# P.V issued for two chunks at a time, four column sums on TensorE, maxima split by reductions alone

## The chip, the cores and the metric

The kernel runs on one core of one Trainium2 chip. The core's engines work side by side and meet only at semaphores: TensorE (PE in the profile, its weight loads PEld), VectorE (DVE), ScalarE (ACT), GpSimd (POOL) and SyncE (SP), which issues the DMAs here. The metric is the time of one execution in device microseconds. Before the change the median of three runs is 5370.73 us (5370.23 to 5371.38).

## The reference

A post-norm transformer layer on x of 4 x 2048 x 512 in fp32, with 16 heads of 32:

```
q, k, v = x @ Wq.T + bq, x @ Wk.T + bk, x @ Wv.T + bv       # 16 heads of 32
scores  = q k^T / sqrt(32) + bias                           # bias: -inf in 3 columns of 2048
attn    = softmax(scores);  ctx = attn @ v
y  = layernorm(x + ctx @ Wo.T + bo) * gamma + beta
x1 = layernorm(x + y)
xq = quantize_4bit(x1 @ Hadamard);  wq = ternary(weight)
out = layernorm(x1 + xq @ wq.T)
```

The part that the change touches is the attention: softmax over 2048 keys for each of 2048 queries, 16 heads and 4 batches.

## The kernel before

Four batches run one after the other. A batch has 4 head groups of 4 heads, and a head group has 4 query blocks of 512 queries, so there are 16 blocks in a batch and 64 in all. After the 16 blocks of a batch comes a phase over its tokens (output projection, norms, quantised layer), which the change does not touch.

One block n works on 16 chunks of 128 keys. For a chunk c and each of the 4 heads, TensorE multiplies keys by queries (`score`, line 491, tile ps_s with NSB = 3 PSUM banks), ScalarE takes the exponential (line 679) into one of NPB = 6 buffers of `prob`, and TensorE adds the product with the values to ps_o (line 518, P.V). The four heads of P.V stand side by side on four strips of 32 columns of the array; scores use its whole width. The scores run one chunk ahead: while chunk c is in hand, the scores of c + 1 are issued, and in chunk 15 those of chunk 0 of the next block.

The sum of the exponentials over all keys is split. For the chunks of `PE_SUMS` TensorE multiplies them by ones (`column_sums`, line 496, ps_z, again on four strips). For the other chunks GpSimd adds the 128 x 2048 exponentials to `acc` (line 994), and at the end of the block TensorE sums `acc` too (the total), which waits for GpSimd's last addition. VectorE then takes the reciprocal (line 816) and GpSimd normalises (lines 978, 981) before it begins the next block's additions. A buffer of `prob` may be written again once its P.V (`pv`) and, for GpSimd's chunks, its addition (`padd`) are done (lines 676, 678).

The exponential needs the maximum of each query's scores before the block begins. So block n also computes the maxima for block n + 1: 64 units (`unit`, line 476), each a product of queries and 512 keys into one of NMB = 3 PSUM banks, of which VectorE takes the maximum (line 803). Unit u waits for the reduction of unit u - 3 (line 473). `unit_places` puts about five units into each of the chunks 1 to 13, one behind each score and two behind the last. Unit 0 waits for the stacked queries of block n + 1 (`q_stk`, line 468). When all 64 are reduced, VectorE combines them to 16 values per query row, negates them and splits them into a rounded high part and a rest (lines 805 to 810, `msplit`); TensorE transposes the two parts (line 483), ScalarE copies them (line 669), and two DMAs put them as rows into the stacked queries (line 321, `q_cur`). They take part in the score product, which so comes out with the maximum subtracted.

In chunk 14 TensorE also projects the queries of block n + 2 (`queries`, line 462, eight matmul records); ScalarE makes the high part (line 665), VectorE the low part (line 783), and SP issues three DMAs that stack them (line 285) and loads for the next projection. In front of the blocks 4, 8 and 12 of a batch (not 12 of the last batch) the keys and values of a head group are projected (lines 430, 436), about 30 us of TensorE. The last block of all has no units, since no block follows.

Every engine has its own program, written by hand in the order in which it runs; the order on TensorE within a block is that of `attend`.

Of the kernel before, what the change touches and what calls it, by code (L numbers as in the profile page):

```python
# [7 lines left out]
ALU = mybir.AluOpType  # L8
ACT = mybir.ActivationFunctionType
AX = mybir.AxisListType  # L10
F32 = mybir.dt.float32
F32R = mybir.dt.float32r
BF16 = mybir.dt.bfloat16

P = 128
NB, L, D = 4, 2048, 512
NH, HD = 16, 32
LBAND = 1024
TOPK = 3
HG = 4  # L20
# [4 lines left out]
NQB = L // QB  # L25
NKC = L // P
# [7 lines left out]
NPB = 6  # L34
# [1 line left out]
NBLK = NG * NQB  # L36
NSB, NMB = 3, 3

PE_SUMS = [2, 5, 8, 11, 14, 15]
POOL_SUMS = [c for c in range(NKC) if c not in PE_SUMS]  # L40
NADD = len(POOL_SUMS) - 1
ADD_OF = {c: max(i - 1, 0) for i, c in enumerate(POOL_SUMS)}
# [62 lines left out]
def build(nc, x, xT, wT, bqkv, woT, w_ffn, band, gamma, beta, bo, had, out):  # L105
# [3 lines left out]
    with ExitStack() as ctx:  # L109
        def sb(name, shape, dt=F32):  # L110
            return ctx.enter_context(nc.sbuf_tensor(name, shape, dt))

        def sem(name):
            return ctx.enter_context(nc.semaphore(name))
# [5 lines left out]
        vst = sb("vst", [P, 2, NKC, P])  # L120
        prob = sb("prob", [P, NPB, HG, QB])
# [8 lines left out]
        hi = sb("hi", [P, 2, QB], F32R)  # L130
        lo = sb("lo", [P, 2, QB], F32R)
        umax = sb("umax", [P, UNITS // NQB, NQB])
        negm = sb("negm", [P, HG * NQB])
        msplit = sb("msplit", [P, 2 * HG * NQB])
        mhi = sb("mhi", [P, HG * NQB], F32R)
        mrow = sb("mrow", [2 * HG * NQB, P], F32R)
        ident = sb("ident", [P, P])
        identb = sb("identb", [P, P], BF16)
# [31 lines left out]
        ps_o = ctx.enter_context(nc.psum_tensor("ps_o", [P, QB], F32))  # L170
# [50 lines left out]
        mstep = sem("mstep")  # L221
        mneg = sem("mneg")
# [3 lines left out]
        ex = sem("ex")  # L226
        pv = sem("pv")
        padd = sem("padd")
        zdone = sem("zdone")
        zrec = sem("zrec")  # L230
        oz_cp = sem("oz_cp")
# [194 lines left out]
        def _(pe):  # L426
# [30 lines left out]
            def queries(f):  # L457

                pe.wait_ge(wq_ld, (f + 1) * 16)
                pe.wait_ge(xq_ld, (f + 1) * 16)  # L460
                for c in range(IC):
                    mm = nc.tensor.matmul(ps_m[:, 0, :], wq[:, c], xq[:, c], start=c == 0, stop=c == IC - 1)  # L462
                mm.then_inc(qproj, 1)

            def unit(u, f, k, stage=None):

                if u == 0:
                    pe.wait_ge(q_stk, (f + 1) * NSTK)
                    if stage is not None:
                        for t in range(2):  # L470
                            pe.wait_ge(k_stk[t], (stage + 1) * (2 * NSTK))
                elif u >= NMB:
                    pe.wait_ge(mred, f * UNITS + u - NMB + 1)
                m, kb = divmod(u, NQB)
                h, qt = divmod(m, QB // P)
                nc.tensor.matmul(ps_m[:, u % NMB, :], qst[k % 2][0:RSTACK, h, qt * P:(qt + 1) * P],  # L476
                                 kst[k // NQB % 2][0:RSTACK, h, kb * QB:(kb + 1) * QB], start=True, stop=True).then_inc(msc, 1)

            def maxima_to_rows(f, first=False):
                if not first:  # L480
                    pe.wait_ge(q_cur, f * 32)
                pe.wait_ge(mneg, f + 1)
                nc.tensor.transpose(ps_m[0:2 * HG * NQB, 1, 0:P], msplit[:], ident[:]).then_inc(mtr, 1)

            def score(n, i, c, h, head=False):

                if c == 0 and h == 0:
                    pe.wait_ge(q_cur, (n + 1) * 32)
                if not head or h >= NSB:
                    pe.wait_ge(ex, n * (HG * NKC) + (HG * c + h - NSB + 1))  # L490
                nc.tensor.matmul(ps_s[:, (i * HG * NKC + HG * c + h) % NSB, :], kst[i // NQB % 2][0:RALL, h, c * P:(c + 1) * P],  # L491
                                 qst[i % 2][0:RALL, h, :], start=True, stop=True).then_inc(sc, 1)

            def column_sums(src, first, last):
                for h in range(HG):
                    mm = nc.tensor.matmul(ps_z[HD * h:HD * h + HD, :], ones[:, 0:HD], src[:, h, :], start=first, stop=last)  # L496
                return mm

            def attend(n, i, last):

                for c in range(NKC):
                    for h in range(HG):
                        if c < NKC - 1:
                            score(n, i, c + 1, h)
                        elif i < NBLK - 1:
                            score(n + 1, i + 1, 0, h)
                        for u in () if last and i == NBLK - 1 else units_at[c][h]:
                            unit(u, n + 1, i + 1, (n >> 2) + 1 if i % NQB == NQB - 1 else None)
                    if c == NKC - 2:
                        if not (last and i == NBLK - 1):  # L510
                            maxima_to_rows(n + 1)
                        if not (last and i >= NBLK - 2):
                            queries(n + 2)
                    if c == 0:
                        pe.wait_ge(oz_cp, n + 1)
                    pe.wait_ge(ex, n * (HG * NKC) + HG * c + HG)
                    for h in range(HG):
                        mm = nc.tensor.matmul(ps_o[HD * h:HD * h + HD, :], vst[:, i // NQB % 2, c, HD * h:HD * h + HD],  # L518
                                              prob[:, c % NPB, h, :], start=c == 0, stop=c == NKC - 1)
                    if c in PE_SUMS:  # L520
                        if c == PE_SUMS[0]:
                            pe.wait_ge(zrec, n + 1)
                        mm = column_sums(prob[:, c % NPB], c == PE_SUMS[0], False)
                    mm.then_inc(pv, 1)
                pe.wait_ge(padd, n * NADD + 2 * NADD)
                column_sums(acc, False, True).then_inc(zdone, 1)

# [79 lines left out]
            for oc in range(IC):  # L607
                mm = nc.tensor.matmul(ps_o[:, oc * P:(oc + 1) * P], ones[:], diag[:, oc * P:(oc + 1) * P], start=True, stop=True)
# [168 lines left out]
        def _(dve):  # L777
# [21 lines left out]
            def maxima(f):  # L799
                for u in range(UNITS):  # L800
                    dve.wait_ge(msc, f * UNITS + u + 1)
                    m, kb = divmod(u, NQB)
                    nc.vector.tensor_reduce(umax[:, m, kb:kb + 1], ps_m[:, u % NMB, :], AX.X, ALU.max).then_inc(mred, 1)  # L803
                dve.wait_ge(mred, (f + 1) * UNITS)
                nc.vector.tensor_reduce(negm[:], umax[:], AX.X, ALU.max, negate=True).then_inc(mstep, 1)
                dve.wait_ge(mstep, f * 2 + 1)
                nc.vector.tensor_copy(mhi[:], negm[:]).then_inc(mstep, 1)
                dve.wait_ge(mstep, f * 2 + 2)
                nc.vector.tensor_copy(msplit[:, 0:HG * NQB], mhi[:].bitcast(F32))
                nc.vector.tensor_tensor(msplit[:, HG * NQB:], negm[:], mhi[:].bitcast(F32), ALU.subtract).then_inc(mneg, 1)  # L810

            def inverse_sums(n):

# [290 lines left out]
```

## Time and profile before

| | |
|---|---|
| median of three runs | 5370.73 us (5370.23 to 5371.38) |
| the profiled execution | 5359.28 us, its span 5357.0 us |
| TensorE | 4980.8 us busy (93%), 25010 matmul records |
| VectorE | 3376.8 us (63%) |
| GpSimd | 3129.3 us (58%), 1103 instructions |
| ScalarE | 2590.8 us (48%) |
| granted TensorE clock | 0.976 of full speed on average; 1.00 in the blocks read below |
| a block without key projection | about 64.1 us from reciprocal to reciprocal |
| a block with it | about 94 to 97 us |
| the last block | 50.0 us |

A row of the timeline gives start and length in us, then engine, line, operation, output and input, the number of instructions merged in the row, and in brackets how long the engine was idle before it and what ended that. A busy TensorE need not be a fast one: where it alternates between kinds of matmul, or waits for a semaphore for a few tenths of a microsecond, the row of busy shares hides it. What a block costs has to be read from the distance between starts. Some matmul records of P.V and the sums count each matmul twice, as two passes.

### The profile page before, as it was taken

The numbers are of one execution on the slowest core, as the hardware profiler recorded it, in microseconds if no ns is written. First come the engines' busy times: TensorE is split into PE (matmuls) and PEld (weight loads), VectorE is DVE, ScalarE is ACT, GpSimd is POOL, SyncE is SP. The second block draws the span as 40 slices with busy tenths as digits, with TensorE's granted clock in tenths as the row PEclk, the third lists the DMA queues.
The fourth block names the chain that finished last, engine by engine and source line by source line (L and its number), as shares of the span: only waits on it lengthen the run. The fifth ranks groups of instructions, "written<-read, shape, count | busy, mean of one in ns | idle before, by whom it ended". The sixth has DMA issues, their size and how long they took to land.

```text
span 5357.0 us, 85355 instructions
## 1 busy us (share of the span) xinstructions
PE 4980.8 (93%) x25010; PEld 2442.2 (46%) x25048; DVE 3376.8 (63%) x5886; ACT 2590.8 (48%) x4891; POOL 3129.3 (58%) x1103
## 2 busy tenths in 40 slices
PE   6999999998889999999879999999988999999987
PEld 3444444443544444454344444444434444444434
DVE  5575756565766575756667666575766757567637
ACT  0454545453555454545345455454534545455545
POOL 1464656565566564656646566564664656566665
PEclk7999999999999999999989999999999999999988
DMA  4414131412411414131341221414133141321112
GB/s 113 93 37 95 37 78 37 95 36 76 112 36 37 95 37 95 37 78 39 89 113 37 51 63 39 93 37 95 37 90 96 36 95 36 72 54 42 36 40 73
DMA packets 247645, 346.36 MB, mean 65 GB/s; under 512 B 16529, under 2 KB 102289, under 8 KB 247186
## 3 DMA queue, kind: packets, MB, share of 16 engines
q1 hardware_dynamic: 247186, 340.73, 27.6%
q8 instruction: 228, 3.74, 0.3%
q14 instruction: 231, 1.89, 0.1%
HBM read 205.33 MB, written 33.55 MB: 45 GB/s over the span
## 4 chain that ended last, share of the span: by engine, by line
PE 74%; DMA 10%; POOL 5%; issue 4%; DVE 3%; ACT 2%; SPq 2%; POOLq 0%; ACTq 0%; DVEq 0%
PE ps_m L476 21%; PE ps_s L491 19%; PE ps_o L518 16%; DMA qst<-lo 7%; PE ps_z L496 5%; PE ps_m L462 4%; PE ps_m L430 3%; PE ps_m L436 2%; DMA xk<-in_xT_dram 2%; SPq L285 1%; ACT prob L679 1%; POOL prob L1020 1%; POOL prob L1024 1%; PE ps_s L436 1%; PE ps_s L430 1%
## 5 line engine op out<-in xcount | busy, mean ns | idle before, releaser
L803 DVE TENSOR_REDUCE umax<-ps_m 128x1 f32<-128x512 f32 x4096 | 2524.9, 683 | 753.3 <-PE ps_m L476 753.3
L679 ACT ACTIVATE prob<-ps_s 128x512 f32<-128x512 f32 x4096 | 2124.6, 601 | 1635.5 <-PE ps_s L491 1470.9
L994 POOL TENSOR_TENSOR acc<-acc,prob 128x2048 f32<-128x2048 f32 x512 | 2344.8, 4580 | 450.9 <-ACT prob L679 421.2
L491 PE MATMUL ps_s<-qst,kst 99*128 99x512 f32 x4096 | 1693.0, 430 | 126.1 <-ACT prob L679 69.4
L476 PE MATMUL ps_m<-kst,qst 97*128 97x512 f32 x4096 | 1699.7, 423 | 35.9 <-DMA qst<-lo 35.9
L491 PEld LDWEIGHTS ps_s<-qst,kst 99*128 99x128 f32 x4096 | 760.7, 190 | 1203.4 <-ACT prob L679 570.1
L518 PE MATMUL ps_o<-prob,vst 128*32 128x512 f32 x8192 | 1094.3, 606 | 0.0
L476 PEld LDWEIGHTS ps_m<-kst,qst 97*128 97x128 f32 x4096 | 780.7, 191 | 475.1 <-DVE umax L803 326.6
L994 POOL TENSOR_TENSOR acc<-prob 128x2048 f32<-128x2048 f32 x64 | 293.0, 4579 | 596.3 <-ACT prob L679 596.3
L978 POOL TENSOR_TENSOR obuf<-obuf,zinv 128x512 f32<-128x512 f32 x64 | 82.1, 1282 | 898.1 <-DVE zinv L816 898.1
L783 DVE SCALAR_TENSOR_TENSOR lo<-ps_m,bias,hi 128x512 fp32r<-128x512 f32 x116 | 87.1, 751 | 616.0 <-ACT hi L665 310.5
L816 DVE RECIPROCAL zinv<-ps_z 128x512 f32<-128x512 f32 x64 | 214.9, 3358 | 354.4 <-PE ps_z L496 354.4
L496 PE MATMUL ps_z<-prob,ones 128*32 128x512 f32 x3072 | 399.9, 592 | 0.0
L542 PE MATMUL ps_s<-vst,hi 128*128 128x512 f32 x512 | 238.5, 610 | 79.8 <-DMA hi<-ctxT_dram 79.8
L518 PEld LDWEIGHTS ps_o<-prob,vst 128*32 128x32 f32 x8192 | 161.9, 108 | 290.8 <-issue 177.0
L462 PE MATMUL ps_m<-xq,wq 128*128 128x512 f32 x512 | 235.7, 603 | 0.7 <-issue 0.7
L430 PE MATMUL ps_m<-xk,wkv 128*128 128x512 f32 x416 | 196.9, 618 | 31.4 <-DMA xk<-in_xT_dram 24.8
L436 PEld LDWEIGHTS ps_m<-wkv,xk 128*128 128x128 f32 x1664 | 194.0, 192 | 25.1 <-issue 25.1
L496 PEld LDWEIGHTS ps_z<-prob,ones 128*32 128x32 f32 x3072 | 99.9, 110 | 229.8 <-issue 229.8
L436 PE MATMUL ps_m<-wkv,xk 128*128 128x128 f32 x1664 | 194.2, 275 | 0.0
L542 PEld LDWEIGHTS ps_s<-vst,hi 128*128 128x128 f32 x512 | 96.4, 197 | 186.4 <-issue 102.1
L647 ACT ACTIVATE hi<-ps_m,bias 128x512 fp32r<-128x512 f32 x52 | 35.7, 687 | 243.0 <-PE ps_m L430 159.1
(105 smaller groups left out, 2341.9 us busy)
## 6 DMA issues: line engine op xcount, KB each, us to landing
xk<-in_xT_dram SPq DMA_DIRECT2D x66, 1024.0 KB, 7.7
xq<-in_xT_dram SPq DMA_DIRECT2D x65, 1024.0 KB, 8.9
kst<-hi SPq DMA_DIRECT2D x128, 256.0 KB, 9.2
qst<-hi SPq DMA_DIRECT2D x128, 256.0 KB, 5.6
wq<-in_wT_dram SPq DMA_DIRECT2D x65, 256.0 KB, 9.2
kst<-lo SPq DMA_DIRECT2D x64, 256.0 KB, 9.1
qst<-lo SPq DMA_DIRECT2D x64, 256.0 KB, 6.8
ctxT_dram<-obuf SPq DMA_DIRECT2D x64, 256.0 KB, 2.5
```

The lines of the kernel that those rows point to most:

```text
L430: mm = nc.tensor.matmul(bank, wkv[:, 0, c], xk[:, t % 2, c], start=c == 0, stop=c == IC - 1)
L436: mm = nc.tensor.matmul(bank[:, u * P:(u + 1) * P], xk[:, t % 2, c, u * P:(u + 1) * P], wkv[:, 1, c], start=c == 0, stop=c == IC - 1)
L462: mm = nc.tensor.matmul(ps_m[:, 0, :], wq[:, c], xq[:, c], start=c == 0, stop=c == IC - 1)
L476: nc.tensor.matmul(ps_m[:, u % NMB, :], qst[k % 2][0:RSTACK, h, qt * P:(qt + 1) * P], kst[k // NQB % 2][0:RSTACK, h, kb * QB:(kb + 1) * QB ...
L491: nc.tensor.matmul(ps_s[:, (i * HG * NKC + HG * c + h) % NSB, :], kst[i // NQB % 2][0:RALL, h, c * P:(c + 1) * P], qst[i % 2][0:RALL, h, : ...
L496: mm = nc.tensor.matmul(ps_z[HD * h:HD * h + HD, :], ones[:, 0:HD], src[:, h, :], start=first, stop=last)
L518: mm = nc.tensor.matmul(ps_o[HD * h:HD * h + HD, :], vst[:, i // NQB % 2, c, HD * h:HD * h + HD], prob[:, c % NPB, h, :], start=c == 0, st ...
L542: nc.tensor.matmul(ps_wo[t % 3], tC[t % 2][:, h * P:(h + 1) * P], wo_sb[:, h, :], start=h == 0, stop=False)
L679: nc.scalar.activation(prob[:, c % NPB, h, :], ps_s[:, (i * HG * NKC + HG * c + h) % NSB, :], ACT.Exp, scale=SCALE).then_inc(ex, 1)
L803: nc.vector.tensor_reduce(umax[:, m, kb:kb + 1], ps_m[:, u % NMB, :], AX.X, ALU.max).then_inc(mred, 1)
L816: nc.vector.reciprocal(zinv[:], ps_z[:]).then_inc(zrec, 1)
L994: nc.gpsimd.tensor_tensor(acc[:], a, prob[:, c % NPB], ALU.add).then_inc(padd, 1)
```

## The change

There are three edits.

P.V is no longer issued in every chunk but in odd ones, for the chunk before and the chunk itself, each followed by its column sums if it is one of `PE_SUMS`. So the scores and units of two chunks stand in a row, and then the strips of two.

`PE_SUMS` shrinks from six chunks to four: 5, 10, 14 and 15. GpSimd takes the other twelve, which are eleven additions instead of nine. The total over `acc` stays on TensorE.

The split of the maxima is made by four reductions in place of a reduction, a cast, a copy and a subtraction: one reduction writes the negated maximum rounded, one writes it in full, one writes the maximum itself rounded, and the last adds the pair of full negated and rounded positive value.

```diff
-PE_SUMS = [2, 5, 8, 11, 14, 15]
+PE_SUMS = [5, 10, 14, 15]
...
-        negm = sb("negm", [P, HG * NQB])
+        mpair = sb("mpair", [P, 2, HG * NQB])
         msplit = sb("msplit", [P, 2 * HG * NQB])
-        mhi = sb("mhi", [P, HG * NQB], F32R)
...
-                    if c == 0:
-                        pe.wait_ge(oz_cp, n + 1)
-                    pe.wait_ge(ex, n * (HG * NKC) + HG * c + HG)
-                    for h in range(HG):
-                        mm = nc.tensor.matmul(ps_o[HD * h:HD * h + HD, :], vst[:, i // NQB % 2, c, HD * h:HD * h + HD],
-                                              prob[:, c % NPB, h, :], start=c == 0, stop=c == NKC - 1)
-                    if c in PE_SUMS:
-                        if c == PE_SUMS[0]:
-                            pe.wait_ge(zrec, n + 1)
-                        mm = column_sums(prob[:, c % NPB], c == PE_SUMS[0], False)
-                    mm.then_inc(pv, 1)
+                    for k in (c - 1, c) if c % 2 == 1 else ():
+                        if k == 0:
+                            pe.wait_ge(oz_cp, n + 1)
+                        pe.wait_ge(ex, n * (HG * NKC) + HG * k + HG)
+                        for h in range(HG):
+                            mm = nc.tensor.matmul(ps_o[HD * h:HD * h + HD, :], vst[:, i // NQB % 2, k, HD * h:HD * h + HD],
+                                                  prob[:, k % NPB, h, :], start=k == 0, stop=k == NKC - 1)
+                        if k in PE_SUMS:
+                            if k == PE_SUMS[0]:
+                                pe.wait_ge(zrec, n + 1)
+                            mm = column_sums(prob[:, k % NPB], k == PE_SUMS[0], False)
+                        mm.then_inc(pv, 1)
...
-                nc.vector.tensor_reduce(negm[:], umax[:], AX.X, ALU.max, negate=True).then_inc(mstep, 1)
-                dve.wait_ge(mstep, f * 2 + 1)
-                nc.vector.tensor_copy(mhi[:], negm[:]).then_inc(mstep, 1)
-                dve.wait_ge(mstep, f * 2 + 2)
-                nc.vector.tensor_copy(msplit[:, 0:HG * NQB], mhi[:].bitcast(F32))
-                nc.vector.tensor_tensor(msplit[:, HG * NQB:], negm[:], mhi[:].bitcast(F32), ALU.subtract).then_inc(mneg, 1)
+                nc.vector.tensor_reduce(msplit[:, 0:HG * NQB].bitcast(F32R), umax[:], AX.X, ALU.max, negate=True)
+                nc.vector.tensor_reduce(mpair[:, 0], umax[:], AX.X, ALU.max, negate=True)
+                nc.vector.tensor_reduce(mpair[:, 1].bitcast(F32R), umax[:], AX.X, ALU.max).then_inc(mstep, 1)
+                dve.wait_ge(mstep, f + 1)
+                nc.vector.tensor_reduce(msplit[:, HG * NQB:], mpair[:].rearrange("p a m -> p m a"), AX.X, ALU.add).then_inc(mneg, 1)
```

The start of a block on TensorE, before: chunk 1's last score, P.V of chunk 0 (L518), the first score of chunk 2, and unit 0 (L476). In brackets stand the semaphores that a row waits for.

```order
L491 MATMUL ps_s<-qst,kst 128x512 [waits ex]
L515 REGISTER_ALU
L518 MATMUL ps_o<-prob,vst 32x512 [waits ex,oz_cp]
L518 MATMUL ps_o<-prob,vst 32x512 x3
L490 REGISTER_ALU
L491 MATMUL ps_s<-qst,kst 128x512 [waits ex]
L468 ISA
L476 MATMUL ps_m<-kst,qst 128x512 [waits q_stk]
```

And after; the lines of `score` and `unit` are one less there.

```order
L490 MATMUL ps_s<-qst,kst 128x512 [waits ex]
L489 REGISTER_ALU
L490 MATMUL ps_s<-qst,kst 128x512 [waits ex]
L467 ISA
L475 MATMUL ps_m<-kst,qst 128x512 [waits q_stk]
```

P.V of chunk 0 no longer stands between the scores of chunk 1 and unit 0; it comes behind the fifth unit, with that of chunk 1.

The end of a block on TensorE, before: the query projection (L462), P.V and sums of chunk 14, the scores of the next block's chunk 0 behind their wait for `q_cur`, P.V and sums of chunk 15, and the total.

```order
L462 MATMUL ps_m<-xq,wq 128x512 x3
L518 MATMUL ps_o<-prob,vst 32x512 [waits ex]
L518 MATMUL ps_o<-prob,vst 32x512 x3
L496 MATMUL ps_z<-prob,ones 32x512 x4
L488 REGISTER_ALU
L490 REGISTER_ALU [waits q_cur]
L491 MATMUL ps_s<-qst,kst 128x512 [waits ex]
L490 REGISTER_ALU
L491 MATMUL ps_s<-qst,kst 128x512 [waits ex] x3
```

And after, from the projection to the total:

```order
L461 MATMUL ps_m<-xq,wq 128x512 x3
L487 REGISTER_ALU
L489 REGISTER_ALU [waits q_cur]
L490 MATMUL ps_s<-qst,kst 128x512 [waits ex]
L489 REGISTER_ALU
L490 MATMUL ps_s<-qst,kst 128x512 [waits ex] x3
L518 MATMUL ps_o<-prob,vst 32x512 [waits ex]
L518 MATMUL ps_o<-prob,vst 32x512 x3
L495 MATMUL ps_z<-prob,ones 32x512 x4
L516 REGISTER_ALU
L518 MATMUL ps_o<-prob,vst 32x512 [waits ex]
L518 MATMUL ps_o<-prob,vst 32x512 x3
```

The wait for `q_cur` now comes directly behind the projection, and all the strips of the block's end stand together.

VectorE at the end of the 64 reductions, after; before, these rows were a reduction, a cast, a copy and a subtraction.

```order
L805 TENSOR_REDUCE msplit<-umax 128x16 [waits mred]
L806 TENSOR_REDUCE mpair<-umax 128x16
L807 TENSOR_REDUCE mpair<-umax 128x16
L809 TENSOR_REDUCE msplit<-mpair 128x16 [waits mstep]
L796 REGISTER_ALU
```

One wait on VectorE's own result is left where there were two.

## Rows read from the trace of the kernel before

**Rows 1.** The page, the chain that ended last, shares of the span by engine:

```profile
PE 74%; DMA 10%; POOL 5%; issue 4%; DVE 3%; ACT 2%; SPq 2%; POOLq 0%; ACTq 0%; DVEq 0%
```

**Rows 2.** Timeline, TensorE, plain chunk: start, length, engine, line, [idle <-releaser]:

```profile
312.14 0.50 PE L491 MATMUL ps_s<-qst,kst 99*128 99x512 f32 x1
...
312.71 0.40 PE L491 MATMUL ps_s<-qst,kst 99*128 99x512 f32 x1
...
312.94 0.40 PE L476 MATMUL ps_m<-kst,qst 97*128 97x512 f32 x1
...
314.25 0.19 PEld L476 LDWEIGHTS ps_m<-kst,qst 97*128 97x128 f32 x1 [0.41 <-DVE umax L803]
...
314.67 1.07 PE L518 MATMUL ps_o<-prob,vst 128*32 128x512 f32 x8
...
315.67 0.19 PEld L491 LDWEIGHTS ps_s<-qst,kst 99*128 99x128 f32 x1 [0.84 <-ACT prob L679]
```

**Rows 3.** Timeline, VectorE: the first 64 units, then two chunks of a block:

```profile
86.91 38.35 DVE L803 TENSOR_REDUCE umax<-ps_m 128x1 f32<-128x512 f32 x64 [13.13 <-PE ps_m L476]
...
308.51 3.08 DVE L803 TENSOR_REDUCE umax<-ps_m 128x1 f32<-128x512 f32 x5 [0.45 <-PE ps_m L476]
...
312.91 3.08 DVE L803 TENSOR_REDUCE umax<-ps_m 128x1 f32<-128x512 f32 x5 [1.32 <-PE ps_m L476]
```

**Rows 4.** The query stack: projections and unit 0 by timeline, then waits (us, times, longest):

```profile
226.75 3.67 PE L462 MATMUL ps_m<-xq,wq 128*128 128x512 f32 x8
...
240.15 0.50 PE L476 MATMUL ps_m<-kst,qst 97*128 97x512 f32 x1 [0.16 <-DMA qst<-lo]
...
355.02 3.67 PE L462 MATMUL ps_m<-xq,wq 128*128 128x512 f32 x8
...
368.74 0.47 PE L476 MATMUL ps_m<-kst,qst 97*128 97x512 f32 x1 [0.51 <-DMA qst<-lo]
...
5062.09 3.61 PE L462 MATMUL ps_m<-xq,wq 128*128 128x512 f32 x8
...
5076.00 0.51 PE L476 MATMUL ps_m<-kst,qst 97*128 97x512 f32 x1 [1.09 <-DMA qst<-lo]
...
PE ps_m L476 <- DMA qst<-lo: 35.9, 49, 13.9
```

**Rows 5.** Timeline, chunks 12 to 14: first scores, the fourth of chunk 14, maxima row:

```profile
346.60 0.50 PE L491 MATMUL ps_s<-qst,kst 99*128 99x512 f32 x1
...
353.19 0.98 PE L491 MATMUL ps_s<-qst,kst 99*128 99x512 f32 x3
...
354.53 0.50 PE L491 MATMUL ps_s<-qst,kst 99*128 99x512 f32 x1 [0.36 <-ACT prob L679]
...
355.47 1.23 SPq L321 DMA_DIRECT2D qst<-mrow  x2
```

**Rows 6.** Timeline, GpSimd: a block's first additions, and the last block's:

```profile
306.84 4.58 POOL L994 TENSOR_TENSOR acc<-prob 128x2048 f32<-128x2048 f32 x1
...
311.49 9.26 POOL L994 TENSOR_TENSOR acc<-acc,prob 128x2048 f32<-128x2048 f32 x2
...
5144.35 37.50 POOL L994 TENSOR_TENSOR acc<-acc,prob 128x2048 f32<-128x2048 f32 x8
```

**Rows 7.** Timeline, the maxima's cast without and with an addition beside it:

```profile
125.54 0.17 DVE L807 CAST mhi<-negm 128x16 fp32r<-128x16 f32 x1
...
345.10 9.23 POOL L994 TENSOR_TENSOR acc<-acc,prob 128x2048 f32<-128x2048 f32 x2 [2.25 <-ACT prob L679]
...
353.42 0.22 DVE L805 TENSOR_REDUCE negm<-umax 128x16 f32<-128x64 f32 x1
353.68 0.69 DVE L807 CAST mhi<-negm 128x16 fp32r<-128x16 f32 x1
```

**Rows 8.** Timeline, a block behind a key projection: exponentials of chunk 1, unit 0:

```profile
460.78 2.06 ACT L679 ACTIVATE prob<-ps_s 128x512 f32<-128x512 f32 x4 [0.93 <-PE ps_s L491]
...
463.19 0.40 PE L476 MATMUL ps_m<-kst,qst 97*128 97x512 f32 x1
```

## The prediction

> **What bounds the kernel now.** I read the page first: the busy shares (TensorE 93%, in the table above) say only who is busy, so I went to the chain that ended last (74% TensorE, 10% DMA) [rows 1], then to the groups by line and the waits, and then to the timeline of one query block. A block (one of 64) takes about 64.1 us, 94 to 97 us where keys of a new head group are projected in front of it, and block n computes both its own attention and the 64 maxima units of block n+1.
>
> Inside a block TensorE alternates between two kinds of work: chunks of scores and units over the whole array (99 and 97 rows), and a burst of P.V on four 32-column strips. A plain chunk is four scores, five units and one burst. [Rows 2] show that it takes 315.67 - 312.14 = 3.53 us, and 3.54 from reduction to reduction. Whole-array matmuls follow each other every 0.235 us (312.71 to 312.94); nine are 2.12 us. The burst starts at 314.67 and the next score at 315.67: 1.00 us. A chunk with column sums takes 312.91 - 308.51 = 4.40 us [rows 3], so four more strips in the same burst cost 0.86 us, and changing kinds costs the rest: 3.54 - 2.12 - 0.86 = 0.56 us per chunk. That 0.56 us is what pairing two chunks hopes to halve.
>
> But part of it is another wait. PSUM has three banks for the units (NMB), so unit u waits for the reduction of unit u-3. In [rows 2] the fifth unit's weights load waits 0.41 us, released by VectorE. VectorE's pace is in [rows 3]: 64 reductions in 38.35 us, the last 0.69 long, so (38.35 - 0.69)/63 = 0.598 us each, with TensorE doing nothing but units there; the runs of five give the same, (3.08 - 0.69)/4. In a block VectorE idles only 0.45 us after a plain chunk and 1.32 us after one with sums [rows 3]: the gap is the burst minus the three reductions that the banks hold back. So the middle of a block is a ring of two engines, not TensorE alone.
>
> The start of a block has a third limit. Unit 0 waits for the stacked queries. Their chain starts when the query projection ends (355.02 + 3.67 = 358.69): ScalarE's high part, VectorE's low part, three DMAs from SP, and unit 0 at 368.74, 10.05 us later; the trace puts this wait down 49 times [rows 4]. Of the blocks, 48 have units and no key projection in front. From the first of them (226.75 + 3.67 to 240.15, 9.73 us) to the last (5062.09 + 3.61 to 5076.00, 10.30 us) the distance is 9.71 to 10.54, on average 9.92. In the last one TensorE's own way there is 0.15 us shorter and the distance is not, so it is the DMA that sets it.
>
> **The change part by part.**
>
> *P.V for two chunks.* Chunks (0,1), (2,3) ... (14,15) now share a burst. Four places differ.
> - Start: P.V of chunk 0, 1.00 us of TensorE, no longer stands ahead of unit 0. Unit 0 stays where the DMA puts it, so TensorE waits about 1.5 us there instead of 0.5, and the 0.86 us of P.V 0 comes behind the fifth unit: **+0.86 us**. The cover that hid this work is what is lost.
> - Pairs (2,3) to (10,11), five of them: ten units in a row. The tenth unit waits for the seventh reduction, five reductions later than the fifth unit's wait, and the scores between them (0.235 us each) fit inside 0.598 us. So a pair is 3.54 + 5 x 0.598 + 0.86 = 7.39 us against 7.08: +0.31 each, **+1.55 us**. The trace has no ten units with scores in between and no burst behind the fifth. Lower bound: no wait for VectorE, 7.08 - 0.56 = 6.52. Upper: the second P.V costs a whole burst, 1.00 for 0.86, 7.53. I take 7.39, from the run of 64 units, which is nearest.
> - Pair (12,13), nine units. Now from the first score of 12 (346.60) to that of 14 (353.19) it is 6.59 us [rows 5]. Then: fifth unit's load 2.12 after the start, four reductions more 2.39, 0.42 to the burst, 1.86 of burst: 6.79. **+0.20 us**.
> - End: the scores of the next block's chunk 0 now come ahead of P.V 14. They wait for the row of maxima (issued from 355.47 to 356.70; TensorE arrives at 358.1, 1.4 us after the last issue), and the fourth waits for an exponential that comes behind the high part, so behind the projection's end at 358.69, and starts near 360.1 [rows 4, 5]. That eats what the saved switch gives. Whatever is left, either way, disappears in the DMA wait of unit 0: 0. No DMA moves against another on SP, and none of SP's waits changes.
>
> *Sums.* Six chunks summed on TensorE become four. Of chunks 2, 5, 8, 11 inside the ring only 5 and 10 remain: 2 x 0.86 = **-1.72 us**. Chunks 14, 15 and the total stay.
>
> GpSimd does eleven additions instead of nine. Two back to back take 9.26 us, 4.63 each. The first starts at 306.84, behind the normalising [rows 6]; eleven end at 357.8 if none waits for an exponential. TensorE asks for the total at about 360.1 + 0.4 + 4 x 0.86 = 363.9, so some 6 us are free, and the exponentials that need a freed buffer come 7 us or more behind the addition that frees it. 0 in 63 blocks. In the very last block there are no units and GpSimd already sets the end: eight additions run without a gap to 5181.85 and the reciprocal follows [rows 6]. There two more cost 2 x 37.50/8 = **+9.4 us once**.
>
> *Maxima by tensor_reduce.* Today the cast takes 0.69 us behind a running addition and ends with it (354.37 against 345.10 + 9.23 = 354.33), and 0.17 us before any addition runs; the plain reduction in front takes 0.22 us beside the same addition [rows 7]. Even so the transpose at 354.77 comes right behind the last score (354.53 + 0.235), so nothing is won by a quicker chain: 0. Its worth is what it avoids, since with twelve chunks GpSimd is adding without a break there. Four reductions are about 0.8 us and end before TensorE arrives (its last burst is 0.86 us longer). A reduction that writes rounded fp32, or one over a pair 16 apart, is in no row: from 0.22 us each as the plain one, to a wait for the running addition, up to 4.6 us. I take the plain one.
>
> The Trainium skill (SBUF — State Buffer, SBUF: two separate sides) says that VectorE in a two-port mode or with two SBUF inputs, and GpSimd, lock one port pair for a whole instruction. VectorE: DVE Perf Modes (the perf-mode tier table) gives tensor_reduce the single-port mode alone. By these the new chain is not held, as I took it; the trace agrees for the cast (0.69 against 0.17) and the plain reduction (0.22).
>
> *The sum.* A block with the DMA wait: 0.86 + 1.55 + 0.20 - 1.72 = +0.89 us; 48 of them, +43. The 15 blocks with new keys or a new batch in front have no such wait: unit 0 comes at 463.19 and would come once the second exponential of chunk 1 ends (460.78 + 1.03, then one score, about 462.25), -0.94 [rows 8]; with the +0.89 that is -0.05 each, -1. Last block +9. Together +51 us on the profiled execution's 5359.28 (its span 5357.0 and 2.3 around it): 5410. The median of the runs is 11.4 us above that execution, so the forecast is 5370.7 + 51 = **5422 us**.
>
> **Rivals.**
> 1. *Pairing pays as meant* (faster). The ring is TensorE's and each pair saves one whole switch of 0.56 us. Per block 6 x 0.56 + 1.72 - 0.86 = 4.2 us, times 48, and some 5.2 in the 15 others, less 9 at the end: 270 us, 5100 us. For it: the 0.56 us is real. Against it: 0.598 us per reduction in every run of units. The 29 reductions that now stand in TensorE's way give the turning point: 0.598 - 0.89/29 = 0.567 us; below that the block is not longer. Chance 0.07.
> A rule speaks for this rival. The Trainium skill (TensorEngine Tiling (Array Packing), Key Properties) says that changing the tiling mode drains TensorE, so half the changes should give half the drains back. The trace agrees that a change costs something (0.84 us before the next load); whether it can be cashed is the question.
> 2. *The stacked queries land sooner* (faster to same). If unit 0 followed TensorE instead of the DMA, the 1.00 us of P.V 0 and the present 0.5 us of wait would come back: 0.89 - 1.5 = -0.6 us in 48 blocks, with the +8 of the rest 5350 us. It decides from a distance of 9.1 us downward; the smallest measured is 9.71. Chance 0.08.
> 3. *The new reductions are held by GpSimd* (much slower). The chain would end with the addition at 357.8 instead of about 355, and TensorE, which comes there at about 355, would stand 2.9 us per block: 63 x 2.9 = 183, 5605 us. Chance 0.04.
> 4. *GpSimd is too slow.* It would need 6 us more per block than [rows 6] give. Chance 0.03, some 5450 us.
> 5. *Smaller terms cancel* (pairs nearer 7.2 than 7.39, end of block better): 5 x 0.19 us x 63 less, 5362 to 5380 us. Chance 0.10.
>
> **How the numbers follow.** The forecast case has the other 0.68; its own range is 5395 to 5445. The range 5378 to 5450 takes in most of case 5 and case 4 and leaves out 1, 2 and 3, at 0.19. Its upper end is the bound of 7.53 us per pair for about half the blocks. A measurement of this kernel can tell 0.2%, 11 us, from no change. Faster: 0.07 + 0.04 (half of case 2) = 0.11, rounded to 0.12. Same: 0.10 + 0.03 = 0.13, less what case 5 lends, 0.12. Slower: 0.76.
>
> **What would show it.** Right: VectorE's runs in a block of 10 reductions, 6.07 us long, with 1.3 us of idle time between (2.2 where chunk 5 or 10 is summed); unit 0 about 9.9 us behind the projection, with 1.5 us of wait for the DMA; from unit 0 to the end of the next projection 55.1 us instead of 54.2; GpSimd in one unbroken run of ten additions; blocks of 65.0 us; a last block near 59 us. Wrong: pairs of 6.6 us with VectorE's idle time under 1 us (rival 1); unit 0 under 9.1 us (rival 2); a reduction of the new chain over 1 us (rival 3); the total waiting for GpSimd in ordinary blocks (rival 4).

## The result, and the profile after

The changed kernel takes 5486.01 us (5480.32 to 5504.23, four runs) against 5370.48 us. The ratio is 1.0224, interval 1.0198 to 1.0250: slower by 2.2%. The direction was forecast, the size was not: +51 us expected, +116 us measured, and 5486 lies above the range's end of 5450.

The profiled execution takes 5490.04 us, its span is 5488.2 us, 131 us longer than before. The chain that ended last, on its page, answers to [rows 1]:

```profile
PE 50%; DVE 16%; issue 15%; DMA 10%; POOL 5%; ACT 2%; SPq 2%; POOLq 0%; DVEq 0%; ACTq 0%
```

VectorE's share went from 3% to 16% and TensorE's from 74% to 50%: the units' reductions now stand on the chain. The timeline of VectorE in one block shows how, and answers to [rows 3]:

```profile
313.73 6.07 DVE L803 TENSOR_REDUCE umax<-ps_m 128x1 f32<-128x512 f32 x10 [1.85 <-PE ps_m L475]
321.12 6.08 DVE L803 TENSOR_REDUCE umax<-ps_m 128x1 f32<-128x512 f32 x10 [1.32 <-PE ps_m L475]
329.38 6.07 DVE L803 TENSOR_REDUCE umax<-ps_m 128x1 f32<-128x512 f32 x10 [2.18 <-PE ps_m L475]
```

Ten reductions in 6.07 us, 1.32 us of idle time behind a plain pair and 2.18 us behind one with a sum; a pair takes 321.12 - 313.73 = 7.39 us. All three were forecast to the hundredth or nearly. The first row has 1.85 us of idle time where 1.3 was expected (and where the next block has 1.32), and that is the first sign of what was missed. TensorE at the start of this block, from unit 0 on (compare [rows 2]):

```profile
307.52 0.50 PE L475 MATMUL ps_m<-kst,qst 97*128 97x512 f32 x1 [1.30 <-DMA qst<-lo]
307.87 0.56 PE L490 MATMUL ps_s<-qst,kst 99*128 99x512 f32 x1
308.22 0.63 PE L475 MATMUL ps_m<-kst,qst 97*128 97x512 f32 x1
308.65 0.63 PE L490 MATMUL ps_s<-qst,kst 99*128 99x512 f32 x1
309.07 0.63 PE L475 MATMUL ps_m<-kst,qst 97*128 97x512 f32 x1
...
310.91 2.12 PE L518 MATMUL ps_o<-prob,vst 128*32 128x512 f32 x16
312.96 0.50 PE L490 MATMUL ps_s<-qst,kst 99*128 99x512 f32 x1
```

And the same place one block later:

```profile
373.83 0.47 PE L475 MATMUL ps_m<-kst,qst 97*128 97x512 f32 x1 [1.52 <-DMA qst<-lo]
374.14 0.39 PE L490 MATMUL ps_s<-qst,kst 99*128 99x512 f32 x1
374.37 0.40 PE L475 MATMUL ps_m<-kst,qst 97*128 97x512 f32 x1
...
376.12 1.92 PE L518 MATMUL ps_o<-prob,vst 128*32 128x512 f32 x16
377.97 0.50 PE L490 MATMUL ps_s<-qst,kst 99*128 99x512 f32 x1
```

The same instructions follow each other every 0.43 us in the first block and every 0.235 us in the second. From unit 0 to the next pair's first score it is 5.44 us against 4.14. The view by stretches says why. Its columns are the stretch, its length, busy time and instructions of TensorE, its loads, VectorE, ScalarE and GpSimd, then the granted TensorE clock, the DMAs' share and GB/s:

```profile
307.50:310.90 3.40, 3.38 (x8) 2.21 (x8) 2.38 (x4) 1.79 (x3) 3.10 (x3) 0.57 0.87 294
...
373.60:377.00 3.40, 3.17 (x17) 1.75 (x20) 2.66 (x5) 1.57 (x3) 3.10 (x3) 1.00 0.86 289
```

Behind unit 0 the granted clock is 0.57, mostly the 1.2 GHz level, in the first block and 1.00, 2.4 GHz, in the second. Over the span it went from 0.976 to 0.956.

I measured the distance from unit 0 to the end of the projection for the 62 blocks that have both. Before, the 14 of the last batch lie at 53.9 to 54.2 us and the others at 54.2 to 54.7, and none is over a microsecond above its fellows. After, the blocks in which the clock stays up lie at 55.04 us in the median, as forecast (55.1). But 42 of the 62 lie at 55.9 to 58.0, together 75.7 us above that. For the profiled execution the forecast was 5410 us and the measurement 5490, and these 75.7 us are nearly all of the 80 between them. (Between the medians, 5422 and 5486, it is 64 us.)

Of the 42 blocks, 33 are among the 47 whose unit 0 waits for the DMA; they make up 63 us. The other nine have no such wait at all. Four of them are the first of a batch, where the granted clock ahead of unit 0 is low already (0.50 to 0.74); five stand behind a key projection, as this one (unit 0 is the third row):

```profile
759.84 0.96 PE L490 MATMUL ps_s<-qst,kst 99*128 99x512 f32 x3 [0.87 <-ACT vst L651]
761.18 1.10 PE L490 MATMUL ps_s<-qst,kst 99*128 99x512 f32 x2 [0.38 <-ACT prob L679]
762.08 0.63 PE L475 MATMUL ps_m<-kst,qst 97*128 97x512 f32 x1
...
762.10:765.50 3.40, 3.40 (x9) 2.27 (x7) 2.27 (x4) 2.78 (x6) 2.82 (x1) 0.53 1.07 300
```

The same block before has the same two idle times, but P.V of chunk 0 stands between them and unit 0, and it kept its clock:

```profile
753.26:756.66 3.40, 3.40 (x18) 1.67 (x17) 2.96 (x5) 2.06 (x4) 3.40 (x1) 1.00 1.05 255
```

So the longer wait at unit 0 is not the whole condition: the microsecond of P.V that is missing there counts as well.

Two more rows answer to terms of the forecast. GpSimd in this block, and in the last block of all, answer to [rows 6]:

```profile
314.39 46.52 POOL L993 TENSOR_TENSOR acc<-acc,prob 128x2048 f32<-128x2048 f32 x10
...
5266.69 46.77 POOL L993 TENSOR_TENSOR acc<-acc,prob 128x2048 f32<-128x2048 f32 x10
```

Ten additions without a break in both, and the last block lasts 59.27 us (reciprocals at 5256.31 and 5315.58) instead of 50.0: the +9.4. The four reductions that split the maxima, beside a running addition, answer to [rows 7]:

```profile
291.82 0.22 DVE L805 TENSOR_REDUCE msplit<-umax 128x16 fp32r<-128x64 f32 x1
291.95 0.21 DVE L806 TENSOR_REDUCE mpair<-umax 128x16 f32<-128x64 f32 x1
292.08 0.21 DVE L807 TENSOR_REDUCE mpair<-umax 128x16 fp32r<-128x64 f32 x1
292.33 0.19 DVE L809 TENSOR_REDUCE msplit<-mpair 128x16 f32<-128x32 f32 x1
```

None of them waits; the longest of the 256 in the run takes 0.22 us.

### The profile page after: what moved, and what is told of

It is laid out like the page before. It is cut to its first block, busy times and chain, and to the rows that moved or that the text cites. A ratio compares the mean times of both kernels' runs of the same rounds, so it can differ in the third digit from the quotient of the medians.

```text
span 5488.2 us, 83623 instructions
## 1 busy us (share of the span) xinstructions
PE 5010.9 (91%) x23986; PEld 2411.8 (44%) x24024; DVE 3322.1 (61%) x5886; ACT 2665.2 (49%) x4891; POOL 3712.9 (68%) x1231
## 3 DMA queue, kind: packets, MB, share of 16 engines
q14 instruction: 234, 1.92, 0.1%
## 4 chain that ended last, share of the span: by engine, by line
PE 50%; DVE 16%; issue 15%; DMA 10%; POOL 5%; ACT 2%; SPq 2%; POOLq 0%; DVEq 0%; ACTq 0%
PE ps_o L518 16%; DVE umax L803 14%; PE ps_m L475 10%; PE ps_s L490 8%; DMA qst<-lo 6%; PE ps_m L461 4%; PE ps_m L429 3%; PE ps_z L495 3%; PE ps_m L435 3%; DMA xk<-in_xT_dram 2%; SPq L284 1%; ACT prob L679 1%; POOL prob L1019 1%; POOL prob L1023 1%; PE ps_s L435 1%
## 5 line engine op out<-in xcount | busy, mean ns | idle before, releaser
L993 POOL TENSOR_TENSOR acc<-acc,prob 128x2048 f32<-128x2048 f32 x640 | 2930.9, 4580 | 75.2 <-ACT prob L679 17.1
L679 ACT ACTIVATE prob<-ps_s 128x512 f32<-128x512 f32 x4096 | 2203.8, 600 | 1574.3 <-PE ps_s L490 1554.2
L475 PE MATMUL ps_m<-kst,qst 97*128 97x512 f32 x4096 | 1894.4, 470 | 113.4 <-DMA qst<-lo 82.4
L475 PEld LDWEIGHTS ps_m<-kst,qst 97*128 97x128 f32 x4096 | 796.2, 194 | 924.2 <-DVE umax L803 767.2
L490 PEld LDWEIGHTS ps_s<-qst,kst 99*128 99x128 f32 x4096 | 779.3, 193 | 802.4 <-issue 509.9
L518 PE MATMUL ps_o<-prob,vst 128*32 128x512 f32 x8192 | 1046.0, 618 | 0.0
L518 PEld LDWEIGHTS ps_o<-prob,vst 128*32 128x32 f32 x8192 | 218.7, 112 | 470.1 <-issue 323.0
L495 PE MATMUL ps_z<-prob,ones 128*32 128x512 f32 x2048 | 267.4, 594 | 0.0
L1001 POOL TENSOR_TENSOR prob<-prob 128x256 f32<-128x256 f32 x64 | 46.7, 729 | 165.9 <-ACT prob L710 165.9
```

The costliest lines, as they stand in the source:

```text
L679: nc.scalar.activation(prob[:, c % NPB, h, :], ps_s[:, (i * HG * NKC + HG * c + h) % NSB, :], ACT.Exp, scale=SCALE).then_inc(ex, 1)
L993: nc.gpsimd.tensor_tensor(acc[:], a, prob[:, c % NPB], ALU.add).then_inc(padd, 1)
```

## The experiments

A stand is a stretch in which TensorE does nothing. Theory A: the forecast's terms are right, and what it left out is the clock: TensorE's longer stand in front of unit 0 lets the granted clock fall, and the first microseconds of the block run at half of it. Its rivals: B, GpSimd without a break costs the rest; C, the pairs further on in the block do.

**e1_unpaired.** Sums and maxima of the change, P.V chunk by chunk.

```diff
-                    for k in (c - 1, c) if c % 2 == 1 else ():
+                    for k in (c,):
```

> The changed kernel with P.V issued chunk by chunk as before: four chunks summed on TensorE, twelve added by GpSimd, the maxima split by reductions. Theory A (pairing lengthens TensorE's stand in front of unit 0, and its clock falls there; the sums pay as forecast): 5370.5 - 63 x 1.72 + 9.4 = 5271 us, the stand stays near 0.5 us and the granted clock stays at full speed in the blocks; from unit 0 to the end of the projection 52.5 us. Theory B (GpSimd's eleven additions without a break are what costs the extra 65 us, not the pairing): the saving is eaten, 5340 us or more, with waits for the additions in ordinary blocks.

Measured: 5267.42 us, ratio to the kernel before 0.9810 (0.9793 to 0.9826). The clock is 0.974. From unit 0 to the projection it is 52.49 us in the median, and one block of 62, the first of a batch, is over a microsecond above the lowest. GpSimd's ten additions run without a break here too (46.47 us), so B falls. The sums alone are a gain of 102 us; the pairing is what costs.

**e2_pair_six_sums.** The pairing alone, with the six sums of before.

```diff
-PE_SUMS = [5, 10, 14, 15]
+PE_SUMS = [2, 5, 8, 11, 14, 15]
```

> The changed kernel with six chunks summed on TensorE again (2, 5, 8, 11, 14, 15), so pairing and the maxima by reductions alone. Theory A: 5486 + 63 x 1.72 - 9.4 = 5585 us, and the clock falls behind the stand at unit 0 as often as in the changed kernel. Theory B: GpSimd has its pauses back and the extra 65 us go, 5520 us.

Measured: 5583.67 us, ratio 1.0392 (1.0375 to 1.0410), with 51 of 62 blocks over a microsecond above the lowest. GpSimd's pauses are back and the extra time is not gone: B falls from this side too. The worth of the sums is nearly the same with the pairing, (97.7 + 9.4)/63 = 1.70 us per block, and without it, (102.3 + 9.4)/63 = 1.77; 1.72 was forecast.

**e3_first_alone.** The changed kernel with P.V of chunk 0 back in front of unit 0.

```diff
-                    for k in (c - 1, c) if c % 2 == 1 else ():
+                    for k in (0,) if c == 0 else (1,) if c == 1 else (c - 1, c) if c % 2 == 1 else ():
```

> The changed kernel, but P.V of chunk 0 and of chunk 1 each in its own chunk again, so that P.V 0 stands ahead of unit 0; pairs from (2,3) on. Theory A: the stand is 0.5 us again, the clock stays at full speed, a block costs 1.55 + 0.20 - 1.72 = +0.03 us against the kernel before: 5370.5 + 2 + 9.4 = 5382 us. Theory C (the clock falls, or time is lost, because of the pairs further on in the block): only the 0.86 us come back, 5486 - 54 = 5432 us, with slow stretches left.

Measured: 5379.22 us, ratio 1.0017 (1.0007 to 1.0026). One block of 62, the first of a batch, is over a microsecond above the lowest, where 42 were. One microsecond of P.V at the right place is worth 107 us in the whole run, and only 41 of them (0.86 us in the 48 blocks that wait for the DMA) are the work itself. The expectation's 54 took the 0.86 in all 63 blocks. The six pairs that are left cost 54.18 - 52.49 = 1.69 us per block against e1_unpaired; 1.75 was forecast. C falls.

**e4_fill.** The changed kernel with work that nobody reads in place of the stand, in all blocks but those whose number in the batch is 4, 8 or 12. All of these 12 but one, the last, have a key projection in front.

```diff
                 if u == 0:
+                    for _ in range(fill):
+                        nc.tensor.matmul(ps_m[:, NMB - 1, :], qst[(k - 1) % 2][0:RSTACK, 0, 0:P],
+                                         kst[(k - 1) // NQB % 2][0:RSTACK, 0, 0:QB], start=True, stop=True)
                     pe.wait_ge(q_stk, (f + 1) * NSTK)
```

> The changed kernel with five extra matmuls of 512 columns (1.2 us of work that nobody reads, into the third unit bank) in front of unit 0's wait in the 48 blocks that have no key projection in front. Theory A: TensorE no longer stands idle there, the clock stays at full speed, unit 0 comes when the DMA lands as before, and from unit 0 to the projection 55.0 us in every block: 5422 us, though work was added. Theory C: no change or a little slower, 5486 to 5500 us.

Measured: 5417.95 us, ratio 1.0090 (1.0073 to 1.0107), for the 5422 of the expectation, which is the forecast itself. TensorE at the start of a block (the fill has line 468, scores 493, units 478):

```profile
303.12 0.99 PE L493 MATMUL ps_s<-qst,kst 99*128 99x512 f32 x2 [0.38 <-ACT prob L683]
303.94 1.31 PE L468 MATMUL ps_m<-kst,qst 97*128 97x512 f32 x5
305.40 0.50 PE L478 MATMUL ps_m<-kst,qst 97*128 97x512 f32 x1
305.74 0.40 PE L493 MATMUL ps_s<-qst,kst 99*128 99x512 f32 x1
305.98 0.40 PE L478 MATMUL ps_m<-kst,qst 97*128 97x512 f32 x1
```

Five matmuls stand where TensorE stood still, unit 0 comes as late as without them (9.81 us behind the projection on average, 9.86 in the changed kernel), and the units behind it are 0.235 us after the scores. Three blocks of 62 are over a microsecond above the lowest, with 3.7 us together instead of 75.7. Added work makes the kernel 68 us faster. The matmuls are the only difference, so it is TensorE's missing work in front of unit 0 that lets the clock fall.

In one block unit 0 waits for the DMA and has no fill in front. It is the only one with this wait that fell:

```profile
4989.12 0.52 PE L478 MATMUL ps_m<-kst,qst 97*128 97x512 f32 x1 [1.06 <-DMA qst<-lo]
...
4989.10:4992.50 3.40, 3.38 (x8) 2.25 (x8) 2.68 (x5) 1.79 (x3) 2.71 (x3) 0.55 0.87 296
```

A stand of 1.06 us, with P.V of chunk 0 gone from in front of it, cost the clock here, and one of 1.09 us behind P.V did not in the kernel before [rows 4].

**e5_old_maxima.** e1_unpaired with the reduction, cast, copy and subtraction of before.

```diff
-                nc.vector.tensor_reduce(msplit[:, 0:HG * NQB].bitcast(F32R), umax[:], AX.X, ALU.max, negate=True)
-                nc.vector.tensor_reduce(mpair[:, 0], umax[:], AX.X, ALU.max, negate=True)
...
+                nc.vector.tensor_reduce(negm[:], umax[:], AX.X, ALU.max, negate=True).then_inc(mstep, 1)
+                dve.wait_ge(mstep, f * 2 + 1)
+                nc.vector.tensor_copy(mhi[:], negm[:]).then_inc(mstep, 1)
...
```

> e1_unpaired (5267 us) with the maxima split as in the kernel before: reduction, cast, copy, subtraction. In e1_unpaired GpSimd adds without a break and the last of the 64 reductions falls about 1.5 us before the end of an addition. Theory P (cast, copy and subtraction each wait for the addition that runs, so the chain needs two additions): the transpose comes some 5 us late in every block, 5267 + 63 x 5 = 5580 us or more with the clock falling at that stand. Theory Q (only the first of them waits, to the end of the running addition): below 1 us per block, 5270 to 5310 us.

Measured: 5599.19 us, ratio 1.0423 (1.0407 to 1.0439): 332 us above e1_unpaired. The timeline of VectorE, TensorE and GpSimd at the end of the reductions:

```profile
338.20 27.83 POOL L995 TENSOR_TENSOR acc<-acc,prob 128x2048 f32<-128x2048 f32 x6
...
359.80 0.22 DVE L806 TENSOR_REDUCE negm<-umax 128x16 f32<-128x64 f32 x1
360.06 1.42 DVE L808 CAST mhi<-negm 128x16 fp32r<-128x16 f32 x1
361.51 0.17 DVE L810 COPY msplit<-mhi 128x16 f32<-128x16 f32 x1
361.59 4.47 DVE L811 TENSOR_TENSOR msplit<-negm,mhi 128x16 f32<-128x16 f32 x1
366.21 0.37 PE L483 MATMUL ps_m<-ident,msplit 128*32 128x128 f32 x1 [4.79 <-DVE msplit L811]
366.46 5.58 PE L462 MATMUL ps_m<-xq,wq 128*128 128x512 f32 x8
```

Additions end at 361.4 and 366.0 there. The cast waits to the first, the copy slips in behind it (0.06 to 0.07 us behind an addition's end in 63 blocks), and the subtraction, with its two inputs in SBUF, waits a whole addition. TensorE stands 4.79 us in front of the transpose, and the projection behind takes 5.58 us instead of 3.67: the clock falls here as well (0.66 granted from 366.4 to 372.1). Theory P holds, with the correction that the copy did not wait. The third edit is no ornament: without it 332 us are lost, against the 102 that the sums gain. (With the pairs the old chain was not run.) It also shows that the engines do not meet only at semaphores, as I wrote ahead of the prediction: VectorE waits here for a running instruction of GpSimd.

The Trainium skill (SBUF — State Buffer, SBUF: two separate sides) has both cases, VectorE in a two-port mode and VectorE with two SBUF inputs, each locked out for a whole GpSimd instruction. The trace agrees: 1.42 us for the cast and 4.47 us for the subtraction, up to an addition's end, and 0.22 us for the reduction.

**e6_maxima_only.** The kernel before with the maxima split by reductions alone (that edit of the change, nothing else).

> The kernel before with the maxima split by reductions alone, nothing else. By the prediction the transpose does not wait for this chain, so 5370 us, the same. Rival: the 0.5 us by which the chain ends sooner reach the row of maxima and the query projection: up to 63 x 0.5, 5340 us.

Measured: 5364.10 us, ratio 0.9996 (0.9987 to 1.0005): the same.

**e7_narrow_reduce.** e3_first_alone with a narrower reduction. It leaves out the last 64 of the 512 scores of each unit from the maxima.

```diff
-                    nc.vector.tensor_reduce(umax[:, m, kb:kb + 1], ps_m[:, u % NMB, :], AX.X, ALU.max).then_inc(mred, 1)
+                    nc.vector.tensor_reduce(umax[:, m, kb:kb + 1], ps_m[:, u % NMB, 0:448], AX.X, ALU.max).then_inc(mred, 1)
```

> e3_first_alone (pairs from (2,3) on, 5379 us) with each unit's reduction over 448 of its 512 columns, about 0.53 us apart instead of 0.598 (it leaves out the last 64 scores of each unit). Ring of three banks: the tenth unit waits for seven reductions, 7 x 0.067 us less in each of five pairs, 6 x 0.067 in (12,13), a little in chunk 1: -2.9 us per block, 5195 to 5215 us. Rival (pairs are bound by TensorE's own work and their reductions only run beside it): less than 20 us, 5360 us.

Measured: 5191.51 us, ratio 0.9669 (0.9654 to 0.9684): 188 us less than e3_first_alone, where the rival gave 20. VectorE in a block:

```profile
320.59 5.40 DVE L803 TENSOR_REDUCE umax<-ps_m 128x1 f32<-128x448 f32 x10 [1.51 <-PE ps_m L475]
327.51 5.40 DVE L803 TENSOR_REDUCE umax<-ps_m 128x1 f32<-128x448 f32 x10 [1.52 <-PE ps_m L475]
```

Ten in 5.40 us and a pair in 327.51 - 320.59 = 6.92 us, 0.47 less than 7.39: seven reductions times 0.067 us, the ring with three banks to the letter. It does not follow that the pairing pays at this pace, for a single chunk gets shorter too: from unit 0 to unit 5, over the unpaired chunk 1, it is 3.51 us here against 3.64 in e3_first_alone, 0.13 or two times 0.067 us less. Two single chunks would then be some 7.08 - 2 x 0.13 = 6.82 us, below the pair's 6.92. That is an estimate; the narrow reduction without pairs was not run.

**e8_three_sums.** e1_unpaired with one more chunk on GpSimd.

```diff
-PE_SUMS = [5, 10, 14, 15]
+PE_SUMS = [8, 14, 15]
```

> e1_unpaired with three chunks summed on TensorE (8, 14, 15) and thirteen added by GpSimd, twelve additions. If TensorE's time alone counts: 63 x 0.86 less, 5213 us. But 12 x 4.65 = 55.8 us of additions begin 5.7 us behind the reciprocal and the total needs them: from reciprocal to reciprocal 62.7 us, above e1_unpaired's 62.2, and TensorE stands in front of the total: 5290 to 5310 us. That is the point from which more additions on GpSimd stop paying.

Measured: 5281.38 us, ratio 0.9841 (0.9826 to 0.9857), 14 us above e1_unpaired. TensorE's loads in front of the total, from the timeline and from the list of waits (us in total, times, longest):

```profile
355.18 0.16 PEld L495 LDWEIGHTS ps_z<-acc,ones 128*32 128x32 f32 x8 [2.46 <-POOL acc L993]
...
PEld ps_z L495 <- POOL acc L993: 128.9, 51, 11.1
```

The total waits for GpSimd in 51 blocks. Less was lost than expected, but 0.86 us per block were not won: of six, four and three chunks on TensorE, four is the best.

**e10_only_first_pair.** e1_unpaired with the pair (0,1) alone.

```diff
-                    for k in (c,):
+                    for k in () if c == 0 else (0, 1) if c == 1 else (c,):
```

> e1_unpaired (5267 us) with one pair alone, (0,1): P.V of chunk 0 goes behind unit 4, all other chunks as in e1_unpaired. Theory A (the clock falls at the lengthened stand in front of unit 0, whatever the rest of the block looks like): 48 x 0.86 = 41 us of moved work and the 65 us of the fallen clock, 5360 to 5385 us, with matmuls 0.43 us apart behind unit 0. Rival (it needs the thinner work of the later pairs too): 5308 us, 5300 to 5315.

Measured: 5376.58 us, ratio 0.9999 (0.9989 to 1.0009). From unit 0 to the projection 45 of 62 blocks are over a microsecond above the lowest, 74 us together; with all pairs it was 42 and 76 us. In one of them the burst of two P.V, 1.92 us at full clock, reads

```profile
240.80 3.10 PE L518 MATMUL ps_o<-prob,vst 128*32 128x512 f32 x16
```

So the first pair alone makes the whole loss of the clock; the later pairs are not needed for it.

This run also parts the length of the stand from what goes ahead of it. It has 21 stands of 1.0 to 1.2 us in front of unit 0, with P.V of chunk 0 moved away, and behind 18 of them the clock fell. The runs that keep P.V of chunk 0 ahead of unit 0 (the kernel before, e1, e3, e5 to e9) have 17 stands of this length together, and behind 2 of them it fell. All runs without it (this one, the changed kernel, e2_pair_six_sums and e4_fill) have 27, and behind 22 it fell.

**e9_last_block.** e1_unpaired with eight chunks on TensorE in the last block, where GpSimd sets the end.

```diff
+LAST_PE = [3, 5, 7, 9, 11, 13, 14, 15]
...
+                end = last and i == NBLK - 1
+                sums, nadd = (LAST_PE, LAST_NADD) if end else (PE_SUMS, NADD)
```

> e1_unpaired with another split of the column sums in the last block of all, where no units run and GpSimd's additions set the end: eight chunks on TensorE, seven additions instead of eleven. Additions: 4 x 4.65 = 18.6 us less, until TensorE's own work decides (16 chunks of 2.4 us and nine groups of 0.86: 46 us against 59.3 now): -13 us, 5254 us, and the best of all. Rival: the token phase behind it is bound by DMAs and takes it back: 5267.

Measured: 5256.08 us, ratio 0.9778 (0.9765 to 0.9792), 11 us below e1_unpaired (13 were expected), and the fastest version that computes the whole of the reference: 2.2% below the kernel before, as far as the change is above it.

## Why the prediction was wrong in size

*The pairs.* Right. 7.39 us per pair was forecast and is in the trace, with the idle times of 1.3 and 2.2 us. e7_narrow_reduce shows the cause, three banks and 0.598 us per reduction. The turning point of 0.567 us that I gave with the first rival is wrong in its working: it holds a single chunk at 3.54 us while the reductions get faster, and e7_narrow_reduce shows one getting shorter.

*The sums.* Right. 2 x 0.86 x 63 - 9.4 = 99 us; e1_unpaired gained 102, and the changed kernel lies 98 below e2_pair_six_sums.

*The last block.* Right: 59.27 us, +9.3.

*GpSimd and the maxima.* Right: no wait in ordinary blocks, and the four reductions take 0.2 us each. e8_three_sums and e5_old_maxima show how near the edge both were.

*The end of the block.* Right to the size of a measurement: unit 0 comes 9.86 us behind the projection on average, 9.92 before. One reading there was off, without harm: in the last of the blocks TensorE's own way is 9.21 us against 9.54 at 368.74 us, so 0.33 us shorter and not 0.15 [rows 4].

*The start of the block.* This is the step that failed. I wrote: "Unit 0 stays where the DMA puts it, so TensorE waits about 1.5 us there instead of 0.5, and the 0.86 us of P.V 0 comes behind the fifth unit: +0.86 us." The stand was sized well (1.42 us on average), and its direct price too: 55.04 us from unit 0 to the projection against 54.18 in e3_first_alone, and e4_fill, which removes only the consequence, comes to 5418 against 5422. But I priced moved work and a stand as time and nothing else. Behind them the clock falls to the 1.2 GHz level in two blocks of three, and the units, scores and the burst that follow take 1.3 us more in many of these, in some 2.7. The term is +0.86 us and +63/47 = 1.3 us on average, 2.2 us in place of 0.86, in the blocks that wait for the DMA. In the 15 others, which I put at -0.05 us each, the clock cost another 13 us together. I had the granted clock of the blocks at 1.00 before and read it as a constant of the kernel, when it was a result of the work that stood in front of unit 0. No row of before showed a fall at that place, so no bound covered it; the range allowed 28 us above the forecast for all terms (7.53 us per pair in 40 of the 63 blocks, more than the half that I named), and this one alone needed 64.

*The rivals.* "Pairing pays as meant" fell: the ring is real. "The queries land sooner" fell: the smallest distance is 9.70 us. "The new reductions are held" and "GpSimd is too slow" fell. What happened was on none of the lists: a cost that grows out of a move and a wait which the sum had counted correctly. That the direction came out as forecast is owed to the terms that were right, which alone made the kernel 0.9% slower (e4_fill); the larger part of the loss was not foreseen.

What stays open is why the clock falls in some blocks and not in others: the block with unit 0 at 307.52 us fell behind a stand of 1.30 us, that at 373.83 us did not behind 1.52. Behind a key projection, without any stand at unit 0, 5 of 11 blocks fell in the changed kernel and none of the same 11 in e4_fill, where they have no fill either. And with P.V of chunk 0 in place the fall is rare, not excluded: none in the kernel before, but one behind 1.10 us in e6_maxima_only.

## What to carry to other kernels

Work in front of a wait that something else bounds can be worth more than its own time: here it also kept TensorE's clock up, so price its removal at the longer stand and at the matmuls behind it at half speed, and if nothing useful can stand there, try matmuls that nobody reads. Before work is batched to save switches, count the buffers between the two engines: a longer run of one kind is paced by the slower engine as soon as the buffers are full, here 7.39 us for a pair against 7.08 for two single chunks. When GpSimd is to run without pauses, first clear VectorE's critical path of casts and of two-input operations from SBUF.

## What the runs showed of the hardware that I had not expected

- The granted clock fell behind stands of 1.1 to 2.2 us in TensorE's work, in 33 blocks of the 47 that have one, and in 5 of 11 blocks without a stand at that place, behind idle times of 0.87 and 0.38 us. The stretch behind unit 0 ran at 0.57 on average of the blocks that fell (matmuls of 512 columns 0.43 us apart instead of 0.235). Five matmuls in the stand prevented it in all 47 filled blocks that wait for the DMA.
- Stands of 1.0 to 1.2 us cost the clock in 22 of 27 cases where a microsecond of P.V was missing ahead of them, and in 2 of 17 where it was there.
- A subtraction of two 128 x 16 tiles took 4.47 us behind a running GpSimd addition, while a copy of the same size directly behind an addition's end took 0.17 us.
- Reductions that write rounded fp32, or read with a stride of 16, take 0.19 to 0.22 us beside a running addition, like a plain one.
